# Storing every operand of a fused attention and feed-forward kernel in split form, once, ahead of the stage that uses it

## The reference

```
xn = layernorm(x)
s  = concat(full_attention(xn), top10percent_attention(xn), memory_head(xn), prediction_head(xn)) @ warboss_w + warboss_b
g  = silu(relu(xn @ w1 + b1) @ w2 + b2)          # w1: 512 x 2048, w2: 2048 x 512
out = x + s * g
```

## Time and profile before

| | us |
|---|---|
| median of 3 runs | 2740.56 |
| lowest and highest run | 2732.62, 2744.57 |
| span of the profiled execution | 2731.8 |
| TensorE busy in the span | 2646.1 |
| VectorE busy | 2415.3 |
| GpSimd busy | 1801.4 |
| ScalarE busy | 1704.5 |

### The profile page before, as it was taken

The page is one execution under the profiler, slowest core; times in us unless marked ns, Lnnn a source line. Parts: engine busy times, 40 slices in busy tenths (PEclk is TensorE's granted clock), DMA queues, the critical chain, the costliest instruction groups (busy, mean ns, idle before and its releaser), DMA issues.

```text
span 2731.8 us, 43928 instructions
## 1 busy us (share of the span) xinstructions
PE 2646.1 (97%) x13537; PEld 2221.8 (81%) x13537; DVE 2415.3 (88%) x5223; ACT 1704.5 (62%) x3038; POOL 1801.4 (66%) x1562
## 2 busy tenths in 40 slices
PE   6999999899999999999999999999999999999997
PEld 5888888677888888888888888887888888888886
DVE  6555555499999999999999999999999999999996
ACT  4565655565666666666666666666666666666664
POOL 2000000176788778877887788778877887788787
PEclk9999999999999999999999999999999999999998
DMA  6333344421222212221222122212221222122212
GB/s 210 136 142 126 128 146 144 142 79 47 62 79 77 68 60 84 72 70 55 85 75 72 55 86 70 70 55 86 71 70 58 86 70 70 59 89 70 70 58 89
DMA packets 224924, 235.24 MB, mean 86 GB/s; under 512 B 13843, under 2 KB 151763, under 8 KB 222677
## 3 DMA queue, kind: packets, MB, share of 16 engines
q1 hardware_dynamic: 224724, 232.75, 26.9%
HBM read 165.59 MB, written 67.11 MB: 85 GB/s over the span
## 4 chain that ended last, share of the span: by engine, by line
PE 66%; DVE 10%; issue 2%; POOL 1%; ACT 1%; DMA 0%; DVEq 0%; POOLq 0%; ACTq 0%; SPq 0%
PE hid L65 7%; PE hid L67 7%; PE hid L66 7%; PE acc L67 7%; PE acc L66 7%; PE acc L65 7%; PE o L1263 6%; PE scores L1249 4%; DVE larger L1152 3%; DVE top_l L1137 2%; PE o L67 2%; PE o L65 2%; PE o L1266 2%; PE o L66 2%; PE scores L67 2%; PE scores L66 2%
## 5 line engine op out<-in xcount | busy, mean ns | idle before, releaser
L975 POOL TENSOR_TENSOR w_lo<-w,w_hi 128x512 fp32r<-128x512 f32 x514 | 685.1, 1354 | 3.9 <-ACT w_hi L823 3.9
L1137 DVE MAX8 top_l<-larger 128x8 f32<-128x512 f32 x832 | 572.8, 688 | 13.2
L1152 DVE MATCH_REPLACE8 larger<-top_l,larger 128x512 f32<-128x512 f32 x768 | 518.5, 675 | 0.0
L975 POOL TENSOR_TENSOR h_lo<-h,h_hi 128x512 fp32r<-128x512 f32 x256 | 341.0, 1332 | 253.2 <-ACT h_hi L860 251.6
L65 PE MATMUL hid<-xnT_hi,w_hi 128*128 128x512 f32 x1024 | 417.4, 408 | 29.5 <-DVE xnT_lo L1177 27.5
L975 POOL TENSOR_TENSOR tl_lo<-tl,tl_hi 128x512 fp32r<-128x512 f32 x65 | 84.2, 1296 | 529.0 <-ACT tl_hi L823 528.4
L67 PE MATMUL hid<-xnT_hi,w_lo 128*128 128x512 f32 x1024 | 402.0, 393 | 0.0
L66 PE MATMUL hid<-xnT_lo,w_hi 128*128 128x512 f32 x1024 | 401.8, 392 | 0.0
L65 PE MATMUL acc<-w_hi,h_hi 128*128 128x512 f32 x1024 | 399.1, 390 | 1.8 <-POOL w_lo L975 1.8
L67 PE MATMUL acc<-w_hi,h_lo 128*128 128x512 f32 x1024 | 400.0, 391 | 0.0
L66 PE MATMUL acc<-w_lo,h_hi 128*128 128x512 f32 x1024 | 399.7, 390 | 0.0
(11 more groups left out here) (164 smaller groups left out, 6182.3 us busy)
## 6 DMA issues: line engine op xcount, KB each, us to landing
w<-in_L_ffn_w SPq DMA_DIRECT2D x260, 256.0 KB, 2.7
xin<-in_L_attn_x SPq DMA_DIRECT2D x18, 1024.0 KB, 6.3
units<-kv_scratch SPq DMA_DIRECT2D x72, 256.0 KB, 3.2
units<-xnT_scratch SPq DMA_DIRECT2D x68, 256.0 KB, 3.2
tl<-tile_scratch SPq DMA_DIRECT2D x65, 256.0 KB, 2.7
xnT_scratch<-xnT SPq DMA_DIRECT2D x16, 1024.0 KB, 8.1
kv_scratch<-kv_out SPq DMA_DIRECT2D x32, 512.0 KB, 2.7
tile_scratch<-tiles_out SPq DMA_DIRECT2D x16, 1024.0 KB, 4.3
```

Of the source, the lines that this page charges most:

```text
L975: return nc.gpsimd.tensor_tensor(out_, value, hi_.bitcast(F32), ALU.subtract).then_inc(ready, 1)
L1137: l_step = count(nc.vector.max(top_l[:, own], larger[:, :]))
L1152: l_step = count(nc.vector.match_replace(larger[:, :], top_l[:, own], larger[:, :], LOWEST))
```

## The change

Each operand is split once, in stage 1, and the two parts are stored side by side in the scratch tensors, which double in size. A new scratch tensor `ffn_d` holds the split w1 and w2 in 16 chunks of 1 MB; each of the 16 halves of stage 1 loads one chunk (w1's 256 KB in runs of 512 bytes and w2's 256 KB in runs of 2 KB), splits it and stores it (1 MB).

In stage 1 ScalarE therefore evicts `ql`, `qs`, `kl`, `ks`, `p2`, `mo`, `v01` and `v23` twice (value and high part), and, behind the evictions of `pi`, waits for the chunk and copies it (128 x 1024). GpSimd, idle in stage 1 before, makes the eight low parts of a half and that of the chunk. SP's program for a half is now: wait for `xn_ready` and load x (1 MB), store the split `xnT` (2 MB), load the w1 and w2 chunk, then store keys (1 MB), the split chunk (1 MB), the tiles (2 MB) and the values (1 MB), each when GpSimd's low part is there. The 4 MB load of w2 is gone. In stage 2 all splits of loaded data are gone, with ScalarE's `hi` and the uses of GpSimd's `lo` and VectorE's `split_xn` for them; TensorE waits for the DMA's semaphores itself. Loads go to rings: four buffers of 1 MB for feed-forward chunks (a load waits for `f2` of the chunk four before), four for tiles, two for the transposed tokens. Keys and values are loaded in pairs of units (1 MB).

The core of the diff:

```diff
-    xnT_d = nc.dram_tensor("xnT_scratch", [2 * B, P, KT, HALF], F32)
-    kv_d = nc.dram_tensor("kv_scratch", [B, P, 8, HALF], F32)
-    tile_d = nc.dram_tensor("tile_scratch", [B * TILES, P, 4, P], F32)
+    xnT_d = nc.dram_tensor("xnT_scratch", [2 * B, P, KT, 2, HALF], F32)
+    kv_d = nc.dram_tensor("kv_scratch", [B, P, 8, 2, HALF], F32)
+    tile_d = nc.dram_tensor("tile_scratch", [B * TILES, P, 2, 4, P], F32)
+    ffn_d = nc.dram_tensor("ffn_scratch", [CH, P, 2, 2, D], F32)
...
@@ stage 1, SP, half n @@
-                        sp.wait_ge(bank_read, KT if first(n) else done(n - 1, "tr3"))
-                        sp.dma_start(xnT_d[bass.ds(n, 1), :, :, :].rearrange("a p k n -> p (a k) n"),
-                                     xnT[:, :, :]).then_inc(xnT_st, 16)
+                        sp.wait_ge(xlo_ready, KT * (n + 1))
+                        sp.dma_start(xnT_d[bass.ds(n, 1), :, :, :, :].rearrange("a p k s n -> p (a k s) n"),
+                                     xnT[:, hh, :, :, :].bitcast(F32).rearrange("p k s n -> p (k s) n")).then_inc(xnT_st, 16)
+
+                        if not first(n):
+                            wait_alone(sp, ffn_st, 16 * n, sp_passed)
+                        raw = ffn[:, LOW, :, :].bitcast(F32)
+                        sp.dma_start(raw[:, W1, :].rearrange("p (k n) -> p k n", n=P),
+                                     w["w1"].rearrange("(k p) n -> p k n", p=P)[:, :, bass.ds(n * P, P)])\
+                            .then_inc(ffn_in, 16)
+                        sp.dma_start(raw[:, W2, :], w["w2"].rearrange("(c p) n -> p c n", p=P)
+                                     [:, bass.ds(n, 1), :].rearrange("p c n -> p (c n)")).then_inc(ffn_in, 16)
...
-                        wait_alone(sp, bank_read, done(n, "ks"), sp_passed)
+                        wait_alone(sp, kv_l, 4 * n + 2, sp_passed)
                         store_kv(0)
...
+                        wait_alone(sp, ffn_l, n + 1, sp_passed)
+                        sp.dma_start(ffn_d[bass.ds(n, 1), :, :, :, :].rearrange("a p s i n -> p (a s i n)"),
+                                     ffn[:, :, :, :].bitcast(F32).rearrange("p s i n -> p (s i n)")).then_inc(ffn_st, 16)
...
@@ stage 1, GpSimd, half n @@
+                        for name, slot in (("ql", T_QL), ("qs", T_QS), ("kl", "kl"), ("ks", "ks"), ("p2", T_PRED),
+                                           ("mo", T_MEM), ("v01", 0), ("v23", 1)):
+                            pool.wait_ge(bank_read, done(n, name))
...
+                            if name == "qs":
+                                pool.wait_ge(ffn_h, n + 1)
+                                left(ffn[:, LOW, :, :], ffn[:, HI, :, :], ffn_l)
...
@@ stage 1, ScalarE, half n @@
-                                    last = nc.scalar.activation(dst, src, ACT.Copy)
+                                    nc.scalar.activation(value, src, ACT.Copy)
+                                    last = nc.scalar.activation(high, src, ACT.Copy)
...
                             last.then_inc(bank_read, 1)
+                            if name == "pi":
+
+                                act.wait_ge(ffn_in, 32 * n + 32)
+                                nc.scalar.activation(ffn[:, HI, :, :], ffn[:, LOW, :, :].bitcast(F32), ACT.Copy)\
+                                    .then_inc(ffn_h, 1)
...
@@ stage 2, SP @@
+                def load_ffn(C, c):
+
+                    if not known_first(C, W_RING):
+                        wait_alone(sp, f2_done, C - W_RING + 1, sp_passed)
+                    sp.dma_start(ffn[:, c % W_RING, :, :, :].bitcast(F32).rearrange("p s i n -> p (s i n)"),
+                                 ffn_d[c % CH, :, :, :, :].rearrange("p s i n -> p (s i n)"))\
+                        .then_inc(ffn_in[c % W_RING], 16)
...
@@ stage 2, TensorE, f1 and f2 @@
-                    pe.wait_ge(w1_l, C + 1)
+                    pe.wait_ge(ffn_in[c % W_RING], (16 // W_RING) * (C - c % W_RING) + 16)
...
-                            pe.wait_ge(xn_l, KT * h + k + 1)
+                            pe.wait_ge(xnT_in[parity][k], 8 * (h - parity) + 16)
...
-                    pe.wait_ge(w2_l, C + 1)
```

More of the change, by code:

```diff
@@ L359, in steps @@
                             elif name in ("ql", "qs", "p2", "mo"):
-                                if name == "ql" and not first(n):
-                                    act.wait_ge(tiles_st, 16 * n)
+                                if name == "ql":
+                                    if first(n):
+                                        act.wait_ge(w_split, KT)
+                                    else:
+                                        act.wait_ge(tiles_st, 16 * n)
                                 slot = {"ql": T_QL, "qs": T_QS, "p2": T_PRED, "mo": T_MEM}[name]
-                                dst = tiles_out[:, :, slot, :]
+                                value = tiles_out[:, :, LOW, slot, :].bitcast(F32)
+                                high = tiles_out[:, :, HI, slot, :]
                                 src = src.rearrange("p (t n) -> p t n", n=P)
@@ L371, in steps @@
                             elif name in ("kl", "ks"):
-                                if name == "kl" and not first(n):
-                                    act.wait_ge(kv_st, 32 * n)
-                                last = nc.scalar.activation(kv_out[:, KV_SLOT[name], :], src, ACT.Copy)
-                            elif name in ("v01", "v23"):
[L377 to L380, removed]
+                                if name == "kl":
+                                    if first(n):
+                                        act.wait_ge(w_split, 2 * KT)
+                                    else:
+                                        act.wait_ge(kv_st, 32 * n)
@@ L595, in _, with stage2 @@
                     steps(b)
-def stage2(nc, x, w, xnT_d, kv_d, tile_d, ident, ww_hi, ww_lo, rows, pick, half_bias, w2, b1, out):
+def stage2(nc, x, xnT_d, kv_d, tile_d, ffn_d, ident, ww_hi, ww_lo, rows, pick, half_bias, b1, out):
     HC = CH // HTILES
     BC = 2 * CH
+    W_RING, TL_RING = 4, 4
     with ExitStack() as ctx:
@@ new lines, in load_kv, with load_xn @@
+                def load_kv(unit, src):
+                    sp.dma_start(kv[:, unit:unit + 2, :, :].bitcast(F32).rearrange("p u s n -> p (u s n)"),
+                                 kv_d[bass.ds(src, 1), :, unit:unit + 2, :, :]
+                                 .rearrange("a p u s n -> p (a u s n)")).then_inc(kv_in[unit], 16)
+                def load_xn(h, parity, src):
+                    if not known_first(h, 2):
+                        wait_alone(sp, f1_done, CH * (h - 1), sp_passed)
+                    for k in range(KT):
+                        sp.dma_start(xnT[:, parity, k, :, :].bitcast(F32).rearrange("p s n -> p (s n)"),
+                                     xnT_d[bass.ds(src, 1), :, k, :, :].rearrange("a p s n -> p (a s n)"))\
+                            .then_inc(xnT_in[parity][k], 16)
```

368 lines of the change are left out of this document (145 added, 223 removed).

## The result

The changed kernel takes 2909.12 us (median of 4 runs, 2908.72 to 2910.45), the kernel before 2740.74 beside it: ratio 1.0618, interval 1.0593 to 1.0643. It is slower by 168 us; forecast were 2920, in 2830 to 2980. The profiled execution has a span of 2907.7 us, 175.9 more than before.

A forecast was written before the change was run, and what follows sets the result against it. TensorE was taken to bound both stages. Span 2731.8 + 208 (stage 1 stall) + 3 (seam) - 31 (stage 2 gain) = 2912, plus 8.8 from span to median: 2920 us, range 2830 to 2980.

The forecast's parts named there:

- Stage 1, the wait: ScalarE's chunk wait behind `pi` stalls TensorE's `wt` 11 us a half; 208 us over 16 halves, clock included.
- S: Start of `mp` in a half of stage 1, from which stall times are counted; 251.28 in the half shown.
- L: Landing of the w1 and w2 chunk behind SP's queue in stage 1, counted from S: 18.3 us.
- L - 7.35: TensorE's stall at `wt` per half of stage 1: L + 6.15 - 13.5, put at 11 us.
- The 0.7 us for w1's short runs: Time added to the chunk's landing L in stage 1 for w1's short runs: 0.7 us.
- The clock: After each stage 1 stall, some 4 us of TensorE work at half speed lose 2 us a half.
- Throughput of stage 1: Extra evictions and copy on ScalarE (94 us) and GpSimd's low parts (13.5 us a half) are hidden.
- The seam: Between the stages, the last values' second eviction, low part and 512 KB more cost 3 us.
- Stage 2's loads: 6.3 MB a slot take 16 us of some 34, with 11 us of cover per chunk load: no cost.
- Stage 2's gain: TensorE's token wait at half starts goes: 27.5 us plus clock, 31 together, ends 27 and 38.
- The offset: Span of the kernel before lies 8.8 us below the median of its runs; added to the forecast span.
- The sum: Whole kernel: 2731.8 + 208 + 3 - 31 = 2912 us of span, 2920 us as median.

The follow-up runs named there:

- e1: Changed kernel with ScalarE's chunk wait and copy, and GpSimd's low part of it, moved from behind `pi` to behind `ks`: 2719.2 us, ratio 0.9907.
- e4: Changed kernel with ScalarE's chunk wait and copy behind `ret`, GpSimd's low part of the chunk behind `ks`: 2696.65 us, ratio 0.9843.
- e2: Changed kernel with the chunk's two loads issued ahead of the x load and the token store: 2767.39 us, ratio 1.0087.
- e3: Changed kernel with one more 1 MB store a half issued ahead of the chunk's loads: 2959.51 us, ratio 1.0786.
- e9: e4 with a second 1 MB HBM-to-HBM transfer ahead of each chunk load in stage 2: 2714.61 us, ratio 0.9903.
- e5: Kernel before, feed-forward using the first half's tokens for all halves, later splits still run; output not the reference's: 2807.76 us, ratio 1.0232.
- e6: e5 also without VectorE's splits of the later halves' tokens; output not the reference's: 2743.92 us, ratio 1.0012.
- e12: e4 with four spare VectorE subtractions of 128 x 512 at the end of each stage 2 half: 2710.97 us, ratio 0.9886.
- e13: e4 with spare VectorE subtractions, ScalarE copies and GpSimd subtractions all given back in stage 2: 2735.03 us, ratio 0.9974.
- e8: e4 with two spare GpSimd subtractions of 128 x 512 in each chunk of stage 2: 2697.83 us, ratio 0.9839.

## Why the prediction was right

**Stage 1, the wait.** Right in place, mechanism and size: 216 us, clock included, where 208 were counted, 13.1 us in the half shown where 13 were. The mean stall is 11.8 us where 11 were counted. The chunk landed at S + 19.3 (S = 390.1) against S + 18.3; the formula L - 7.35 gives 12.0 us from that, and 12.0 were measured. The 0.7 us for w1's short runs in L is shown by no run; with it the landing came 1.0 us after L, without it 1.7. Of the steps to L, the x load was issued at S + 5.9, not S + 4.1, and the chunk 2.3 us later than counted; that showed little, since the queue was still busy with tiles and values. e1 and e4 show the wait's place by removing the loss, e2 and e3 show the queue by the byte.

**The clock.** Counted 2 us a half, measured 1.7, (216.2 - 188.3) / 16: the half clock lasts 3.5 us beyond the stall on average, not 4.

**Throughput of stage 1.** Costed at nothing, and e4 shows it: stage 1 ends less than 1 us later than before. GpSimd's low part of the chunk took 3982 ns, not the 2.7 us counted, without effect.

**The seam.** 3 counted, 3.4 measured.

**Stage 2's loads.** Costed at nothing. TensorE waits 4.3 us for chunks, and e9 doubles their traffic for 18 us.

**Stage 2's gain.** The term that was mis-sized: 31 us (27 to 38), measured 43.7. I took the wait of the earlier trace rows as the whole loss. The earlier trace rows already had VectorE busy for 2088 of 2130 us, 98%; I read it as "next", and said that nothing that is only taken off ScalarE or GpSimd can shorten stage 2, so that GpSimd's lighter load would be without effect. e5 and e6 show that without the token wait VectorE is late elsewhere, at the gates above all; e12 and e13 show that most of the gain is VectorE's lighter load, its own splits (14 us) and, with them, its neighbours' (24 us). The 14 are for splits of 0.69 us each, as e12 gives them back; beside the old GpSimd load they took 1.31, so that a part of the 24 is theirs. How the 24 divide between GpSimd and ScalarE was not tried: no run gives VectorE's splits back with one of the two alone. The trace of e13 speaks for GpSimd.

**The offset.** I added 8.8 us from span to median; the kernel after has 1.4. The runs of both kernels that have a span on record are some 1.8 us longer than it; the rest of the 8.8 is most likely that the profiled execution of the kernel before was a fast one, among runs of 2730 to 2756 us. If so, the 43.7 is counted against a fast execution too.

**The sum.** 8 and 0.4 us too little, 12.7 and 7.4 too much: 11 us above the 2909. The errors are of opposite signs, so that it came this close is in part luck.

## What to carry to other kernels

When work is moved to an earlier stage, price first where its wait stands in a strictly ordered engine: here work that is free by throughput cost 212 us behind one eviction and nothing behind another nine jobs later. Count the landing from all bytes ahead in the queue. And read a second engine at 98% of a stage as a second bound: here, removing the wait that showed (e5, e6) gained nothing, and what counted was how much that engine had to do, with what its neighbours' instructions added to its own.

## What the runs showed of the hardware that was not expected

- VectorE's subtraction of two 128 x 512 operands takes 680 ns alone and 1775 with a GpSimd subtraction beside it all the way (e6); the 128 x 1024 operation on `prob` takes 1285 ns in the kernel after and had a mean of 1800 in the kernel before. e8, by adding GpSimd work alone, raises its median to 1719.
- GpSimd's low part of 128 x 1024 in place takes 3982 ns in each half (3975 to 3995), where 128 x 512 in place takes 1283. It is not the size alone: GpSimd's low parts of 128 x 1024 at the start of stage 1, which go to another tile (`wp_lo`), take 2.5 us. Why this one takes three times what 128 x 512 takes stays open.
